# Gated cross-attention with router and experts, one core: row bands of 32 on TensorE for scores and row maxima, turned copies of keys and queries, and four pieces of work at other places

## What is computed

```
def _L0_xattn_ref(queries, keys, values, Wq, bq, Wk, bk, Wv, bv, Wo, bo):
    q = _split_heads(queries @ Wq + bq)          # 8 heads x 4
    k = _split_heads(keys @ Wk + bk)
    v = _split_heads(values @ Wv + bv)
    scores = jnp.einsum('bhqd,bhkd->bhqk', q, k) * scale
    attn = jax.nn.softmax(scores, axis=-1)
    o = jnp.einsum('bhqk,bhkd->bhqd', attn, v)
    return o.transpose(0, 2, 1, 3).reshape(b, s, h * hd) @ Wo + bo

x = x + jnp.tanh(g_xattn[0]) * _L0_xattn_ref(_layernorm(x), ctx_1024, ctx_1024, ...)
x = x + jnp.tanh(g_ffn[0]) * _L0_ffn_ref(_layernorm(x), router_w, router_b, w1, b1, w2, b2)
```

## Time and profile before

| | us |
|---|---|
| median of 3 runs | 595.37 (594.85 to 595.54) |
| the profiled execution, its own time | 594.75 |
| its span | 592.9 |
| prologue, up to the first qfull copy | 47.3 |
| attention units 0 to 15, up to the last osb copy | 297.5 |
| router search and experts, the rest | 248.0 |

### The profile page before, as it was taken

The page is one execution under the profiler, slowest core; times in us unless marked ns, Lnnn a source line. Parts: engine busy times, 40 slices in busy tenths (PEclk is TensorE's granted clock), DMA queues, the critical chain, the costliest instruction groups (busy, mean ns, idle before and its releaser), DMA issues.

```text
span 592.9 us, 12821 instructions
## 1 busy us (share of the span) xinstructions
PE 551.4 (93%) x5043; PEld 318.6 (54%) x5043; DVE 444.1 (75%) x811; ACT 397.4 (67%) x774; POOL 196.8 (33%) x193
## 2 busy tenths in 40 slices
PE   6798899998999989999999998899999999999994
PEld 4433333333333333333333344469889898898974
DVE  3889879996798967989897258746767868677541
ACT  2587789987888878898888830044665646655651
POOL 3058030024420063400158010240735626346234
PEclk9999999999999999999999999999999999999998
DMA  8600000000000000000000004122735556356133
GB/s 280 241 2 1 1 1 3 2 1 38 2 36 2 2 37 1 37 2 1 37 38 2 36 19 140 34 60 72 163 112 117 144 136 148 108 107 163 16 36 35
DMA packets 23807, 35.80 MB, mean 60 GB/s; under 512 B 3459, under 2 KB 16196, under 8 KB 23620
## 3 DMA queue, kind: packets, MB, share of 16 engines
q1 hardware_dynamic: 17604, 26.59, 13.8%
q0 software_dynamic: 6144, 8.39, 8.3%
HBM read 26.59 MB, written 8.39 MB: 59 GB/s over the span
## 4 chain that ended last, share of the span: by engine, by line
PE 67%; DVE 18%; ACT 5%; issue 4%; POOL 3%; DMA 1%; POOLq 0%; ACTq 0%; DVEq 0%; SPq 0%
PE ps L1719 15%; PE ps L1726 15%; PE ps L1488 12%; DVE mquart L1016 11%; PE ps L1475 6%; PE ps L1454 6%; PE ps L1384 2%; ACT probs L741 2%; PE ps L1345 2%; POOL xn L528 2%; PE ps L1360 1%; PE ps L1697 1%; PE ps L1672 1%; ACT osb L641 1%; PE ps L1513 1%
## 5 line engine op out<-in xcount | busy, mean ns | idle before, releaser
L1016 DVE TENSOR_REDUCE mquart<-ps 128x2 f32<-128x802 f32 x256 | 241.9, 988 | 33.4 <-PE ps L1454 30.2
L741 ACT ACTIVATE probs<-ps 128x512 f32<-128x512 f32 (+1 forms) x416 | 222.9, 599 | 24.0 <-PE ps L1475 20.8
L1488 PE MATMUL ps<-probs,vp 128*32 128x256 f32 (+1 forms) x1664 | 132.7, 391 | 4.5 <-ACT osb L641 4.5
L1454 PE MATMUL ps<-kpad,qrows 64*128 64x401 bf16 x512 | 90.6, 337 | 3.7 <-DVE mquart L1016 3.1
L1475 PE MATMUL ps<-qfull,kpad 64*128 64x256 bf16 (+1 forms) x832 | 89.8, 272 | 2.8 <-ACT x L762 0.9
L1313 DVE TENSOR_TENSOR h1l<-hf,h1h 128x512 fp32r<-128x512 f32 x64 | 44.4, 693 | 56.0 <-ACT hf L868 56.0
L867 ACT ACTIVATE h1h<-ps,b1T 128x512 fp32r<-128x512 f32 x64 | 44.0, 687 | 53.8 <-PE ps L1719 53.6
L1726 PE MATMUL ps<-w2h,h1h 128*128 128x256 f32 x256 | 73.8, 288 | 2.2 <-DVE h1l L1313 1.5
L1726 PE MATMUL ps<-w2l,h1h 128*128 128x256 f32 x256 | 72.4, 283 | 0.0
L1726 PE MATMUL ps<-w2h,h1l 128*128 128x256 f32 x256 | 72.3, 283 | 0.0
L1475 PEld LDWEIGHTS ps<-qfull,kpad 64*128 64x128 bf16 (+1 forms) x832 | 38.9, 96 | 48.2 <-ACT probs L741 25.1
(11 more groups left out here) (198 smaller groups left out, 682.3 us busy)
## 6 DMA issues: line engine op xcount, KB each, us to landing
w1raw<-in_L_ffn_w SPq DMA_DIRECT2D x16, 512.0 KB, 4.6
w2raw<-in_L_ffn_w SPq DMA_DIRECT2D x16, 512.0 KB, 4.7
xs<-in_x SPq DMA_DIRECT2D x4, 512.0 KB, 7.7
ctx_sb<-in_ctx SPq DMA_DIRECT2D x3, 512.0 KB, 5.8
out<-xs SPq DMA_DIRECT2D x3, 512.0 KB, 2.6
x_rows<-x SPq DMA_DIRECT2D x3, 512.0 KB, 2.6
b2b<-in_L_ffn_b SPq DMA_DIRECT2D x1, 1024.0 KB, 11.1
out<-xs SPq DMA_DIRECT2D x2, 256.0 KB, 2.0
```

Source lines behind the costliest of these rows:

```text
L741: nc.scalar.activation(out_p, ps[0:w, next_bank(), :], ACT.Exp, scale=float(SCALE)).then_inc(s_ex, 1)
L1016: nc.vector.tensor_reduce(mquart[:, u % 2, t, a, :, kq], ps[:, b:b + 2, 0:MAXW], AX.X, ALU.max).then_inc(s_mr, 1)
L1454: last = mm(ps[:, bank + b, 0:MAXW], qrows[band(b), g, q:q + P], kpad[band(b), g, a, lo:lo + MAXW], start=True, stop=True)
L1488: last = mm(ps[32 * hh:32 * hh + 32, PV, 0:UW], vp[0:w, kt, g, hh, :], probs[0:w, step % PROBS, hh, :], start=(kt == 0), stop=(kt == NKT - 1))
```

## The change

Scores and maxima get row bands of 32 partitions, one head each. With `band` gone, `score_band(p)` is partitions 0 to 63 in two bands and `max_band(b)` is 64 to 127 in two bands. `kpad` and `krows` give way to `kbands`, the unmasked key rows, and `kturned`, the same with the two halves of the partitions exchanged; the weight columns are spread so that heads 0, 2, 1, 3 stand in the four bands (`places`, `place_of`). `qturned` holds the lower half of the query rows in the upper partitions. The turned copies are made by transfers that SP issues: two for each key block, one for each group of queries of a chunk. They come ahead of the loads of b2b, w1 and w2, and in the loop over chunks between the store of x1 and that of x2.

A maximum tile is a pair of bands as before, but the tiles run over both query tiles of heads in the upper partitions first, then over those of the turned ones. `scores` reserves both banks first and then goes p = 0, p = 1, p = 0, p = 1. `place_max` puts both halves of the heads into partitions 0 to 63 of one bank, side by side, and ScalarE copies 64 x 512 values instead of 128 x 256.

The masks for kpad go (two products on VectorE for each block of group 0, two on ScalarE for each of group 1). From chunk 1 on, c1 and c2 of the queries are made by GpSimd (`split_queries`). The statistics of the first layer norm for chunks 2 and 3 move from r = 0 of the chunk before, steps 0 to 3, to steps 9 to 12 of units 1 and 5; those of the second move from (1, 2) to (1, 5) to (1, 4) to (1, 7). The output projection moves from (0, 10) to (0, 12), the second transpose of x2 from (2, 8) to (2, 7), the router from (2, 10) to (2, 9). Beside this the weights are spread over their columns with fewer, larger copies.

```diff
-        kpad = ar("kpad", [P, NG, 2, KEYS], BF16)
+        kbands = ar("kbands", [P, NG, KEYS], BF16)
+        kturned = ar("kturned", [P, NG, KEYS], BF16)
...
-        qfull = ar("qfull", [P, NG, CW], BF16)
+        qturned = ar("qturned", [P, NG, 2, CW], BF16)
+        qfull = ar("qfull", [P, NG, 2, CW], BF16)
...
-        krows = ar("krows", [P, 2, CW], BF16)
...
-        def band(p):
-
-            return slice(64 * p, 64 * p + 64)
+        def score_band(p):
+
+            return slice(32 * p, 32 * p + 32)
+
+        def max_band(b):
+
+            return slice(64 + 32 * b, 64 + 32 * b + 32)
+
+        def place_of(head):
+
+            return 2 * (head % 2) + head // 2
...
-        O_THIS, O_LAST, BACK_AT, WO_AT = (2, 4), (0, 4), (0, 7), (0, 10)
+        O_THIS, O_LAST, BACK_AT, WO_AT = (2, 4), (0, 4), (0, 7), (0, 12)
         XN_AT, Q_AT = ((0, 9), (0, 11)), ((1, 3), (1, 6))
-        X2_AT, ROUTER_AT = ((2, 6), (2, 8)), ((2, 10), (2, 12))
+        X2_AT, ROUTER_AT = ((2, 6), (2, 7)), ((2, 9), (2, 12))
...
-        LN1_AT, LN2_AT = ((0, 0), (0, 1), (0, 2), (0, 3)), ((1, 2), (1, 3), (1, 4), (1, 5))
+        LN1_AT = {(u, NKT - CT + t): (c, t) for c, u in ((2, 1), (3, PER_CHUNK + 1)) for t in range(CT)}
+        LN2_AT = ((1, 4), (1, 5), (1, 6), (1, 7))
...
+            def turn_keys(j, g):
+
+                lo, w = KB[j]
+                sp.wait_ge(s_rows, BLOCKS.index(("k", j, g)) + 1)
+                sp.dma_start(kturned[64:P, g, lo:lo + w], kbands[0:64, g, lo:lo + w]).then_inc(s_kup[g], 16)
+                sp.dma_start(kturned[0:64, g, lo:lo + w], kbands[64:P, g, lo:lo + w]).then_inc(s_kdown[g], 16)
+
+            def turn_queries(c, g):
+
+                sp.wait_ge(s_rows, rows_of(c, g))
+                if c > 1:
+                    sp.wait_ge(s_mm, TILES * (PER_CHUNK * (c - 2) + PARTS * (g + 1)))
+                sp.dma_start(qturned[64:P, g, c % 2, :], qrows[0:64, g, CW * c:CW * c + CW]).then_inc(s_qt[NG * (c % 2) + g], 16)
+
+            for g in range(NG):
+                for j in range(4):
+                    turn_keys(j, g)
+                turn_queries(0, g)
+            sp.dma_start(b2b[:, :, :], b2.rearrange("e h -> (e h)").partition_broadcast(P)).then_inc(s_b2, 16)
             for half in range(2):
                 load_w1(0, half)
                 load_w2(0, half)
-            with sp.Fori(0, LAST) as c:
+            for g in range(NG):
+                turn_queries(1, g)
+            for c in range(LAST):
                 sp.wait_ge(s_x1, c + 1)
-                sp.dma_start(out_v[:, bass.ts(c, CT), :], xs[:, bass.ts(c, CT), :]).then_inc(s_out1, 16)
+                sp.dma_start(out_v[:, CT * c:CT * c + CT, :], xs[:, CT * c:CT * c + CT, :]).then_inc(s_out1, 16)
+                if c + 2 < NC:
+                    for g in range(NG):
+                        turn_queries(c + 2, g)
                 sp.wait_ge(s_x2, c + 1)
-                sp.dma_start(x2_v[:, bass.ts(c, CT), :], x2[:, :, :]).then_inc(s_x2st, 16)
+                sp.dma_start(x2_v[:, CT * c:CT * c + CT, :], x2[:, :, :]).then_inc(s_x2st, 16)
...
-                pool.wait_ge(s_kpad0, 4)
-                at_least(pool, s_kpad1, b - 1)
-                split_rows(pool, nc.gpsimd, 5 + b, w, krows[:, b % 2, 0:w])
+                split_rows(pool, nc.gpsimd, 5 + b, w, kbands[:, 1, lo:lo + w])
...
+
+            def split_queries(c, g, n):
+
+                pool.wait_ge(s_t1, n)
+                pool.wait_ge(s_xf, n + 1)
+                nc.gpsimd.tensor_scalar(c1[:, :], xf[:, g, :], cst[:, C_MASK:C_MASK + 1], None, ALU.mult).then_inc(s_c1, 1)
+                split_rest(pool, nc.gpsimd, n, g, CW)
+                pool.wait_ge(s_t1, n + 1)
+                nc.gpsimd.tensor_scalar(c2[:, :], t1[:, :], cst[:, C_MASK + 1:C_MASK + 2], None, ALU.mult).then_inc(s_c2, 1)
+                split_rows(pool, nc.gpsimd, n, CW, qrows[:, g, CW * c:CW * c + CW])
...
-                        split_rest(pool, nc.gpsimd, n + g, g, CW)
-                        split_rows(pool, nc.gpsimd, n + g, CW, qrows[:, g, CW * (c + 1):CW * (c + 2)])
+                        split_queries(c + 1, g, n + g)
...
-                at_least(act, s_t1, n)
+                at_least(act, s_t1, n if n < len(BLOCKS) else n - 1)
...
-                nc.scalar.activation(c1[:, 0:w], ps[:, bank, 0:w], ACT.Identity, bias=biasneg[:, col:col + 1],
-                                     scale=cst[:, mask:mask + 1]).then_inc(s_c1, 1)
+                if n < len(BLOCKS):
+                    nc.scalar.activation(c1[:, 0:w], ps[:, bank, 0:w], ACT.Identity, bias=biasneg[:, col:col + 1],
+                                         scale=cst[:, mask:mask + 1]).then_inc(s_c1, 1)
                 nc.scalar.activation(xf[:, half, 0:w], ps[:, bank, 0:w], ACT.Identity, bias=bias).then_inc(s_xf, 1)
...
-            def pad_k1(j):
-
-                lo, w = KB[j]
-                act.wait_ge(s_rows, 5 + j + 1)
-                for b in range(2):
-                    last = nc.scalar.activation(kpad[:, 1, b, lo:lo + w], krows[:, j % 2, 0:w], ACT.Copy,
-                                                scale=cst[:, C_HEAD + b:C_HEAD + b + 1])
-                last.then_inc(s_kpad1, 1)
...
-                    pad_k1(j - 1)
...
-            pad_k1(3)
...
-                take(qfull[:, g, UW * h:UW * h + UW], ps[:, next_bank(), 0:UW], s_qf)
+                take(qfull[0:64, g, :, UW * h:UW * h + UW], ps[0:64, next_bank(), :].rearrange("p (v q) -> p v q", v=2), s_qf)
...
-                    if c + 1 < NC and (r, kt - 2) in Q_AT:
-                        split_middle(NKB + NG * (c + 1) + Q_AT.index((r, kt - 2)), "q", CW)
...
-                split(j, j % 2, w, 2, krows[:, j % 2, 0:w])
-                dve.wait_ge(s_rows, j + 1)
-                for b in range(2):
-                    last = nc.vector.tensor_scalar(kpad[:, 0, b, lo:lo + w], krows[:, j % 2, 0:w],
-                                                   cst[:, C_HEAD + b:C_HEAD + b + 1], None, ALU.mult)
-                last.then_inc(s_kpad0, 1)
+                split(j, j % 2, w, 2, kbands[:, 0, lo:lo + w])
...
-                t, a, kq = j // (2 * QUARTERS), j // QUARTERS % 2, j % QUARTERS
+                a, t, kq = 1 - j // (UQ * QUARTERS), j // QUARTERS % UQ, j % QUARTERS
...
-                    if 0 < c < LAST and (r, kt) in LN1_AT:
-                        ln1_stats(c + 1, LN1_AT.index((r, kt)))
-                    if 0 < c < LAST and (r, kt - 1) == LN1_AT[-1]:
-                        ln1_aggr(c + 1)
+                    if (u, kt) in LN1_AT:
+                        ln1_stats(*LN1_AT[u, kt])
+                    if kt == 0 and (u - 1, NKT - 1) in LN1_AT:
+                        ln1_aggr(LN1_AT[u - 1, NKT - 1][0])
...
-                t, a, kq = j // (2 * QUARTERS), j // QUARTERS % 2, j % QUARTERS
+                a, t, kq = 1 - j // (UQ * QUARTERS), j // QUARTERS % UQ, j % QUARTERS
                 if j == 0 and h == 0:
                     pe.wait_ge(s_rows, rows_of(c, g))
-                if n < 4:
-                    pe.wait_ge(s_kpad0, n + 1)
+                if n == 0:
                     pe.wait_ge(s_xf, 4)
-                if (c, g, h, j) == (0, 1, 0, 0):
-                    pe.wait_ge(s_kpad1, 4)
+                if a == 0 and h == 0 and j == UQ * QUARTERS:
+                    if c == 0:
+                        pe.wait_ge(s_kup[g], 64)
+                    pe.wait_ge(s_qt[NG * (c % 2) + g], 16 * (c // 2 + 1))
                 bank = next_dve((s_mr, n + 1))
-                lo, q = MAXSTEP * kq, CW * c + UW * h + P * t
+                lo, q = MAXSTEP * kq, UW * h + P * t
                 for b in range(2):
-                    last = mm(ps[:, bank + b, 0:MAXW], qrows[band(b), g, q:q + P], kpad[band(b), g, a, lo:lo + MAXW], start=True, stop=True)
+                    rows = max_band(b)
+                    queries = qrows[rows, g, CW * c + q:CW * c + q + P] if a else qturned[rows, g, c % 2, q:q + P]
+                    keys = (kbands if a else kturned)[rows, g, lo:lo + MAXW]
+                    last = mm(ps[:, bank + b, 0:MAXW], queries, keys, start=True, stop=True)
                 last.then_inc(s_mm, 1)
...
-                mm(ps[:, bank, 0:UW], ident_bf[:, :], qrows[:, g, q:q + UW], start=True, stop=False, skip_group_check=True)
-                for t in range(UQ):
-                    last = mm(ps[:, bank, P * t:P * t + P], mparts[:, t, :, :].rearrange("p h r -> p (h r)"), ident_bf[:, :],
-                              start=False, stop=True, skip_group_check=True)
+                for v in range(2):
+                    mm(ps[0:64, bank, UW * v:UW * v + UW], ident_bf[:, 64 * v:64 * v + 64], qrows[:, g, q:q + UW],
+                       start=(v == 0), stop=False, skip_group_check=True)
+                    for t in range(UQ):
+                        last = mm(ps[0:64, bank, UW * v + P * t:UW * v + P * t + P], mparts[:, t, 2 * v:2 * v + 2, :].rearrange("p h r -> p (h r)"),
```

(26 more changed lines are left out.)

40 lines of the change are left out of this document (18 added, 22 removed).

## The result

| | before | after |
|---|---|---|
| median of the runs | 595.41 us | 608.01 us (605.33 to 609.28) |
| profiled execution, its span | 594.75, 592.9 | 607.57, 605.8 |
| up to the first qfull copy | 47.3 | 47.4 |
| attention, up to the last osb copy | 297.5 | 309.0 |
| the rest | 248.0 | 249.4 |

The change makes the kernel slower: ratio 1.0206, 95% interval 1.0175 to 1.0236. The prediction said 582.2 us, 574.5 to 591.5; it missed by 26 us and in its sign. The loss lies in the attention, +11.5 us. A run more than 1.5% above the fastest of its kernel counts as slow and is left out of ratios, while medians and ranges hold all runs.

What follows compares the result with a forecast made beforehand. The prediction saw VectorE, TensorE and ScalarE all full in quiet units, with VectorE's reads remaining the bound. Its terms, chiefly layer norm 6.6 us, summed to 13.2 us off the median 595.37: 582.2 us, range 574.5 to 591.5.

Steps and rivals of the forecast that it cites:

- stands at 1.00, the upper of its two levels, in all of them: Attention units of the kernel before: TensorE's clock read as full in every listed window; no price set for losing it.
- Rival (c): Score matmuls: awaiting both banks first makes it slower; about 600 us if the second half comes 0.25 us late; chance 0.08.
- The bands' gain: Score and maximum matmuls overlap, saving 46 us of TensorE; VectorE bounds quiet units, so only 0.1 us each for 3, 7, 11.
- units 6 and 10: Units r2: with 16 x 0.18 us off TensorE, VectorE's 16.3 plus 0.8 of stalls; gain 1.2 us each.
- Units 4 and 8: First layer norm moved out, no wait for xn: 18.9 us, a gain of 3.3 us each, bounds 2.4 and 4.8.
- Unit 5: Query projection plus moved statistics: 17.3 + 1.5 + 2.5 = 21.3 us, less 0.2 of lost pauses, so 0.2 us worse.
- Unit 9: Query projection with c1 and c2 off ScalarE: busy 17.3, gaps 1.4 + 1.1, so 19.8 us, gain 1.1.
- Unit 1: Query projection plus moved statistics: 15.76 + 1.5 + 2.8 = 20.0 us, gain 0.9.
- Unit 12: Last chunk's r0 unit, 18.46 us before, already without the first layer norm: gain 0.35 us.
- GpSimd's c1 and c2: Query groups on GpSimd: 1.8 us per operation (1.16 to 2.45), 5.9 a group, hidden before x2's transposes.
- The turned copies: SBUF-to-SBUF transfers of turned keys and queries: land in 2.0 us, in time; cost zero, bounds 0 and 1.
- The prologue's 0.6 us: Before attention: dropping VectorE's mask products lets ScalarE's c1 of the first queries come earlier; gain 0.6 us.

Runs made afterwards that it cites:

- the extra matmuls in units r0 and r1: Changed kernel, GpSimd's last weight block held back, a useless 128-row matmul in steps 4 to 12 of units r0 and r1: 599.68 us (593.50 to 610.14).
- GpSimd held back: Changed kernel, but GpSimd's last block of expert weights waits until the last unit's maxima are split: 604.9 us, ratio 1.0177.
- bank by bank: One bank awaited, both halves scored, then the other: 603.67 us on the changed kernel; 595.42 with only its bands, other places as before.
- the moves alone: Kernel before (64-row bands, masked keys) with moved statistics, output projection, transposes and router, and c1 and c2 of queries on GpSimd: 592.35 us, ratio 0.9943.
- the repaired kernel: Changed kernel with scores bank by bank and GpSimd's last weight block held back, no extra matmuls: 592.0 us (586.0 to 597.7), ratio 0.9882.
- both banks first: Kernel before (64-row bands) with the changed kernel's score order, both banks awaited, then halves alternating: 603.35 us, ratio 1.0147.
- 128 rows in the extra matmuls: Changed kernel, bank by bank, GpSimd's last weight block held back, 36 useless 128-row matmuls in units r0: 587.6 us, ratio 0.9881.
- 32 rows: The same kernel as with 128 rows, but its 36 extra matmuls use 32 rows: 590.5 us, ratio 0.9917.
- the first pair: Changed kernel with a useless matmul in all attention steps but one per unit: 607.66 us with 128 rows, 624.3 us with 32.

## Why the prediction was wrong

**The clock.** The step that failed first is a sentence: the clock "stands at 1.00, the upper of its two levels, in all of them". That was true of the kernel before and was carried over to a kernel that gives TensorE other work, with no bound and no rival. Its price is the difference to the same unit, with both banks awaited too, in a profiled run in which the clock stayed up: unit 2 1.7 us (18.30 for 16.59), unit 5 2.9 (23.56 for 20.67), unit 6 1.0, unit 9 2.9 (22.59 for 19.72), unit 13 1.1, unit 15 1.0, unit 1 0.2, and 1.4 in the rest; some 12 us. Unit 5 undisturbed, with the extra matmuls in units r0 and r1:

```profile
144.75:165.42 20.67, 19.53 (x213) 7.03 (x210) 17.56 (x35) 15.89 (x32) 15.64 (x14) 1.00 0.09 34
```

**Both banks.** Rival (c) had the mechanism and, at 0.08, too small a chance. The reason against it was that a group needs 0.47 us from the freeing exponential to its own, against 0.56 of the one that runs. That sum takes TensorE as free when the bank comes free. It isn't: probs·V or a maximum pair stands ahead in its queue, and in the step shown above the 0.47 were 0.56. No late second half was needed. Its price was 8.0 us in the kernel before; in the changed one it is 7.5, unit by unit, with 0.46 in each quiet unit and nothing in units 0, 1, 5 and 9. The rival's own price was off too: 0.25 us late is 0.16 a step, 33 us in 208 steps, which gives 615 and not 600. The forecast needed the bank-by-bank order, where quiet units do take 15.2 us, as it said.

**VectorE and GpSimd.** The sum had no term for it. The two-input operation behind GpSimd's run, and the stretch at 1.2 GHz behind it, cost 3.9 us in unit 14 (22.13, 18.26 with GpSimd held back). The trace before had it in a small form, 0.81 us where the others took 0.20, in the same unit. I read only mean durations of this group, never its maximum.

**The bands' gain.** Right in the quiet unit only by its size of 0.1 (0.17 measured, bank by bank). Too large in units 6 and 10, where I took 1.2: bank by bank they take 17.8 and 17.5 us for 18.4, and 0.1 to 0.3 of that came with the moves alone (18.3, 18.1). TensorE stays the busiest there, 17.26 of 17.77 us in unit 6 (17.98 before): its busy time fell by 0.7 us, where the prediction had 16 x 0.18 = 2.9 for the overlap.

**The rest of the sum** can be judged in undisturbed units. Units 4 and 8: 19.9 us for 18.9, 19.2 bank by bank; the wait for xn is gone (0.17 us), the one ahead of the output projection's copy is 0.83 for 1.04. Unit 5: 20.7 for the predicted 21.1. Unit 9: 19.7 to 19.9 for 19.8. Unit 1: 20.4 to 20.6 for 20.0. Unit 12: 17.8 bank by bank, 18.1 predicted. GpSimd's c1 and c2 took 1.56 to 1.57 us each for my 1.8, inside the bounds, and x2 was hidden: complete at 170.79, its transposes at 176.08. (Twice the 1.21 us is 2.42, where the bound says 2.45; nothing hangs on it.) The turned copies landed in 2.0 us and nobody waited. The prologue's 0.6 us didn't come: the queries' c1 waits 1.28 us for the projection, which ends no earlier (24.89).

```profile
24.93 0.78 ACT L693 ACTIVATE c<-ps,biasneg,cst 128x512 bf16<-128x512 f32 x1 [1.28 <-PE ps L1407]
```

With what failed put in, the sum is 582.2 + 12.0 (clock) + 7.5 (banks) + 3.9 (unit 14) = 605.6, and 2.4 short of 608.0. These are the terms just named, units 6, 10, 4, 8, 1, 0 and the prologue: undisturbed and bank by bank, the units add up to 10.5 us less than before, an estimate of 584.9 us, 2.7 above the forecast. The best run of the repaired kernel took 586.0, with a mean clock of 0.986 where the kernel before has 0.996.

## What to carry to other kernels

Where a change lowers what TensorE has to do, price the loss of its clock as a case of its own, even if TensorE isn't the bound: here a query projection in such a stretch took 3.78 us for 1.98, and its unit 2.9 us more. An order that waits for two buffers before the first use of one is not free because a duration fits under another; ask what stands ahead in the same queue at the time the buffer comes free. And look at the longest, not the mean, of the short operations.

## What the runs showed of the hardware

**The clock fell where TensorE was busier than in places where it stayed up.** With the 32-row bands it fell at 145.3 and 298.9, behind units with these rows:

```profile
125.29:145.30 20.01, 18.12 (x220) 7.36 (x216) 16.58 (x23) 17.44 (x35) 1.73 (x1) 1.00 0.00 1
280.31:298.90 18.59, 16.62 (x210) 6.45 (x208) 16.13 (x22) 16.08 (x32) 1.78 (x1) 1.00 0.00 1
```

TensorE is busy 91 and 89% there, and its longest wait is 0.87 us. In the last 3.3 us ahead of the first of these falls it is busy 2.48 us, 75%:

```profile
142.00:145.30 3.30, 2.48 (x34) 0.83 (x34) 2.86 (x4) 3.23 (x7) 1.73 (x1) 1.00 0.01 2
```

With 64-row bands, at 85% (19.05 of 22.39 us, unit 4 with both banks first) and with a wait of 1.44 us (before, 135.55), it stayed at 2.4 GHz; from 132.2 to 135.6 TensorE was busy there for 1.96 of 3.40 us, 58%. The Trainium skill, TensorE: Matmul & The Clock Gate, section HAM oscillation, puts such falls down to waits in which TensorE stands idle; here that does not tell these units apart, and the measurement decides. In unit 14 of the moves alone the trace agrees: with 64-row bands too the clock fell, at 323.4, behind a wait of 2.59 us for mparts. With 128 rows in the extra matmuls the clock was low for 3.4 us of the attention, with 32 rows for 20.5; in the first pair for 10.2 and 59.2. Why the rows matter stays open: the 32-row matmuls also lie in rows that the scores use.

**A VectorE operation with two inputs in SBUF can wait for a whole run of GpSimd's instructions**: 3.03 to 4.00 us in five kernels (4.00, 3.66 and 3.18 in the changed one, the moves alone and the changed one bank by bank), 0.20 in the moves alone once GpSimd paused.
